# Expert stage of an audio-tower kernel: expert rows ordered by copy then expert, and the bias product cut to a quarter of the tokens per quarter tile

## The reference

```
gate_logits = x @ gate_w + gate_b
topk_vals, topk_idx = top_k(gate_logits, 2);  topk_w = softmax(topk_vals)
h = relu(einsum('bsh,ehf->bsef', x, w1) + b1)        # 16 experts x 128 hidden
expert_out = einsum('bsef,efh->bseh', h, w2) + b2
moe = sum over the two chosen experts of topk_w * expert_out
y = layernorm(x + moe) * gamma + beta
```

## Time and profile before

| | us |
|---|---|
| median of 3 runs (lowest, highest) | 782.41 (780.72, 784.95) |
| the profiled execution's own time | 780.68 |
| its span, first to last instruction | 778.5 |
| PE busy | 741.2 (95%) |
| PE weight loads busy | 435.2 (56%) |
| DVE busy | 579.5 (74%) |
| ACT busy | 492.1 (63%) |
| POOL busy | 459.6 (59%) |

### The profile page before, as it was taken

How to read it: one execution, slowest core, us unless ns; L and a number is a source line. 1 busy time by engine, 2 the same in 40 slices (tenths; PEclk the granted TensorE clock), 3 DMA queues, 4 the chain that set the end, 5 groups by cost and what they waited for, 6 DMA issues and landing times.

```text
span 778.5 us, 17037 instructions
## 1 busy us (share of the span) xinstructions
PE 741.2 (95%) x5712; PEld 435.2 (56%) x5712; DVE 579.5 (74%) x1474; ACT 492.1 (63%) x993; POOL 459.6 (59%) x620
## 2 busy tenths in 40 slices
PE   2999999999999999999999999999999999999994
PEld 1343356776667667676766666544555554454441
DVE  7676776677677676777767665788888888888864
ACT  1566777777767777777777777554554655545441
POOL 7645314654556445564446542367788788888885
PEclk9999999999999999999999999999999999999997
DMA  6300205455755466454664557000000000000000
GB/s 177 105 2 2 53 3 133 110 123 118 160 120 119 106 140 157 109 123 110 145 143 100 117 124 160 2 2 1 9 13 10 9 9 8 8 16 7 9 7 20
DMA packets 41820, 56.20 MB, mean 72 GB/s; under 512 B 16360, under 2 KB 40680, under 8 KB 41608
## 3 DMA queue, kind: packets, MB, share of 16 engines
q1 hardware_dynamic: 40744, 53.87, 30.0%
q10 hardware_dynamic: 992, 1.26, 0.6%
HBM read 5.06 MB, written 2.43 MB: 10 GB/s over the span
## 4 chain that ended last, share of the span: by engine, by line
PE 82%; DVE 4%; POOL 4%; issue 3%; SPq 3%; ACT 3%; DMA 2%; ACTq 0%; DVEq 0%; POOLq 0%
PE bank L1446 14%; PE bank L1424 13%; PE bank L1316 13%; PE bank L1274 10%; PE bank L1343 8%; PE bank L1345 6%; PE bank L1187 5%; PE bank L1278 2%; PE bank L1177 2%; DMA m<-s2o 1%; PE bank L1471 1%; SPq L333 1%; PE bank L1463 1%; PE bank L1230 1%; ACT cs L624 1%
## 5 line engine op out<-in xcount | busy, mean ns | idle before, releaser
L953 DVE TENSOR_SCALAR prob<-prob,cap_hi,cap_lo 125x500 f32<-125x500 f32 x256 | 152.6, 623 | 84.8 <-ACT prob L668 83.7
L478 POOL TENSOR_TENSOR sq<-sq 125x256 f32<-125x256 f32 x128 | 97.5, 773 | 194.2 <-ACT sq L632 172.3
L668 ACT ACTIVATE prob<-bank 125x500 f32<-125x500 f32 x256 | 149.6, 596 | 56.4 <-PE bank L1345 55.8
L1424 PE MATMUL bank<-cs,w_sb 64*64 64x500 f32 x1024 | 147.1, 580 | 2.2 <-DVE gated L1071 2.0
L1446 PE MATMUL bank<-gated,w_sb 64*64 64x500 f32 x1024 | 148.9, 588 | 0.0
L522 POOL TENSOR_TENSOR gated<-relu,wb 128x500 f32<-128x500 f32 x96 | 120.1, 1253 | 48.0 <-ACT relu L768 45.6
L1071 DVE SCALAR_TENSOR_TENSOR gated<-bank,nb,wb 128x500 f32<-128x500 f32 x160 | 114.8, 727 | 35.2 <-PE bank L1424 35.2
L768 ACT ACTIVATE relu<-bank,b_sb 128x500 f32<-128x500 f32 x96 | 64.7, 673 | 93.2 <-PE bank L1424 93.2
L1424 PEld LDWEIGHTS bank<-cs,w_sb 64*64 64x64 f32 x1024 | 53.1, 133 | 54.7 <-issue 48.2
L632 ACT ACTIVATE sq<-bank 125x512 f32<-125x512 f32 x128 | 75.3, 599 | 3.9 <-POOL sq L478 0.8
L1274 PE MATMUL bank<-wqku_hi,s 128*125 128x512 f32 x192 | 77.1, 401 | 0.0
(11 more groups left out here) (188 smaller groups left out, 1507.1 us busy)
## 6 DMA issues: line engine op xcount, KB each, us to landing
m1o<-cs SPq DMA_DIRECT2D x128, 125.0 KB, 2.4
m<-mlow SPq DMA_DIRECT2D x120, 125.0 KB, 2.3
m1e<-cs SPq DMA_DIRECT2D x112, 125.0 KB, 2.4
out<-res SPq DMA_DIRECT2D x15, 125.0 KB
w_sb<-in_w SPq DMA_DIRECT2D x1, 1024.0 KB
m1e<-m1e SPq DMA_DIRECT2D x8, 125.0 KB, 2.3
xa<-xparts SPq DMA_DIRECT2D x3, 281.2 KB
w_sb<-in_w SPq DMA_DIRECT2D x1, 512.0 KB
```

Source lines behind the costliest of these rows:

```text
L478: gp.tensor_tensor(sq2[q][:, :, :], sq[q][:, :, 0:D // 2], sq[q][:, :, D // 2:D], ALU.add)\
L668: act.activation(prob[v % PROBS][:, :, c, :], bank[5 + n % 3][0:T, 0:C].rearrange("p (h l) -> p h l", h=2), ACT.Exp).then_inc(b_exp, 1)
L953: dve.tensor_scalar(part, part, cap_hi[0:T, h:h + 1], cap_lo[0:T, h:h + 1], ALU.min, ALU.max)\
L1424: last = pe.matmul(up_bank(g)[cols, 0:C], w1_sb[rows, g, cols], cs1[q % 3][rows, :], start=True, stop=True)
```

## The change

The 128 rows of a group are ordered copy first, then expert: row 16r + e. That changes the layout of `w1`, `b1`, `w2` and `b2` on the host and the broadcast with which DVE writes `wtok`. At the end of the attention stage PE sums `b2f` once over the 8 copies, with a 0/1 matrix of 128 columns that is added to the table of constants. The result, `b2s`, has the full bias of the 16 experts in rows 0 to 15 and again in rows 64 to 79, and zeros in the other rows. In each half, the first 16 rows of `wb` hold the weights of the 16 experts once. Each half of the rows can now make the full bias product, so each of the four tiles gets a quarter of the tokens (125 columns): rows LO tokens 0 to 249, rows HI tokens 250 to 499.

```diff
-C_COLS = C_II + D
+C_SUM = C_II + D
+C_COLS = C_SUM + 128
...
+    for half in (0, HALF):
+        c[:, C_SUM + half:C_SUM + half + E] = np.tile(np.eye(E), (R, 1))
...
+        b2s = sb("b2s", [128, D])
-        wtok = sb("wtok", [T, CH, E, R])
+        wtok = sb("wtok", [T, CH, R, E])
...
 ACT, start_c:
+                if v == 2:
+                    act.wait_ge(c_bsum, 1)
+                    act.activation(b2s[:, :], bank[4][:, 0:D], ACT.Copy).then_inc(c_bias, 1)
...
 DVE, gate_step, n == 17:
-                    first, second = (lg[:, k, :, :].unsqueeze(3).to_broadcast([T, CH, E, R]) for k in (5, 6))
+                    first, second = (lg[:, k, :, :].unsqueeze(2).to_broadcast([T, CH, R, E]) for k in (5, 6))
                     done(dve.tensor_tensor(wtok[:, :, :, :], first, second, ALU.add))
...
 PE, start_c:
                 if v == 1:
                     pe.wait_ge(b_ev, 16 * PAIRS)
                     pe.wait_ge(b_gl, 4 * PAIRS)
+                    pe.matmul(bank[4][:, 0:D], c_sb[:, C_SUM:C_SUM + 128], b2f[:, :], start=True, stop=True)\
+                        .then_inc(c_bsum, 1)
+                    pe.wait_ge(b_gl, 4 * PAIRS)
                     tokens_c(0)
...
 PE, extra:
                 pe.wait_ge(c_wbs, q + 1)
-                for cols, part in ((LO, slice(0, L)), (HI, slice(L, C))):
-                    for rows, y in ((LO, bank[0]), (HI, bank[1])):
-                        pe.matmul(y[cols, part], b2f[rows, :], wb[q % 2][rows, part], start=False, stop=False,
-                                  skip_group_check=True)
+                if q == 0:
+                    pe.wait_ge(c_bias, 1)
+                for c, (cols, rows, y) in enumerate(((LO, LO, bank[0]), (HI, LO, bank[0]), (LO, HI, bank[1]), (HI, HI, bank[1]))):
+                    part = slice(c * T, (c + 1) * T)
+                    pe.matmul(y[cols, part], b2s[rows, :], wb[q % 2][rows, part], start=False, stop=False,
+                              skip_group_check=True)
...
 host:
-    w1 = a("L0_ffn_w1").reshape(E, D, G, R)
+    w1 = a("L0_ffn_w1").reshape(E, D, G, R).transpose(1, 2, 3, 0).reshape(D, G, 128)
...
-        "b1": a("L0_ffn_b1").reshape(E, G, R).transpose(0, 2, 1).reshape(128, G),
-        "w2": a("L0_ffn_w2").reshape(E, G, R, D).transpose(0, 2, 1, 3).reshape(128, G, D),
-        "b2": np.repeat(a("L0_ffn_b2"), R, axis=0),
+        "b1": a("L0_ffn_b1").reshape(E, G, R).transpose(2, 0, 1).reshape(128, G),
+        "w2": a("L0_ffn_w2").reshape(E, G, R, D).transpose(2, 0, 1, 3).reshape(128, G, D),
+        "b2": np.tile(a("L0_ffn_b2"), (R, 1)),
```

More of the change, by code:

```diff
@@ L173, in build @@
         s_wprod = sem("s_wprod")
+        c_bsum, c_bias = sem("c_bsum"), sem("c_bias")
         a_xin, a_split, a_scr, a_table = sem("a_xin"), sem("a_split"), sem("a_scr"), sem("a_table")
@@ L1471, in weights_c @@
                     last = pe.transpose(bank[3][:, c * T:(c + 1) * T],
-                                        wtok[:, c, :, :].rearrange("p e r -> p (e r)"), ident[0:T, 0:T])
+                                        wtok[:, c, :, :].rearrange("p r e -> p (r e)"), ident[0:T, 0:T])
                 last.then_inc(c_wt, 1)
@@ L1568 @@
         "gb": rows(a("L0_ffn_gate_b"), T),
-        "w1": np.tile(w1.transpose(1, 2, 0, 3).reshape(D, G, 128), (2, 1, 1)),
-        "b1": a("L0_ffn_b1").reshape(E, G, R).transpose(0, 2, 1).reshape(128, G),
-        "w2": a("L0_ffn_w2").reshape(E, G, R, D).transpose(0, 2, 1, 3).reshape(128, G, D),
-        "b2": np.repeat(a("L0_ffn_b2"), R, axis=0),
+        "w1": np.tile(w1, (2, 1, 1)),
+        "b1": a("L0_ffn_b1").reshape(E, G, R).transpose(2, 0, 1).reshape(128, G),
+        "w2": a("L0_ffn_w2").reshape(E, G, R, D).transpose(2, 0, 1, 3).reshape(128, G, D),
+        "b2": np.tile(a("L0_ffn_b2"), (R, 1)),
         "fg": rows(a("L0_ffn_gamma"), T),
```

## The result

The kernel after takes 787.73 us (median of 8 runs, 785.03 to 789.91), the kernel before 782.26 in 8 runs. The ratio is 1.0064, 95% interval 1.0044 to 1.0084. The forecast was 779.7 us, 776.8 to 782.8. The change makes the kernel slower by 5.5 us, not faster by 2.7.

A forecast was written before the change was run, and what follows sets the result against it. The prediction took PE to bound the steady expert stage. 14 pairs at 0.21 us gave -2.9 us, the larger table +0.2, together -2.7: 779.7 us against a median of 782.41, range 776.8 to 782.8.

The forecast's parts named there:

- The smaller `extra`: PE's bias product in the expert stage: half the columns, 0.21 us instead of 0.42, gaining 0.21 us a pair.
- rival (a): Expert stage: short `extra` instructions are limited by their weight loads; gain 0.15 us a pair, 780.7 us; chance 0.13.
- serial rival (d): Tiles of short `extra` don't overlap, weight loads run one after another: 0.64 us more a pair, 791 us; chance 0.02.
- The sum: Whole kernel: -2.9 us from the pairs plus 0.2 us at the start gives -2.7 us.
- the count of pairs: Expert stage: the gain reaches the end in 14 pairs, 1 to 13 and the last.
- The start, the new steps, the new order: Larger constants table costs 0.2 us at the start; new steps ending attention and the new row order cost zero.
- What is late next: Steady pairs: PE's third `up` behind `extra` keeps 0.12 us, the `wtok` transposes 0.45 us; cost taken as nothing.
- Rival (c): DVE and POOL collide in each steady pair, delaying PE's third `up` by 0.84 us: +7 us, 789.6; chance 0.05.
- The argument on pairs 0 and 14: PE stalls there behind `extra` (0.96 and 1.08 us) waiting for a bank DVE must read, so nothing is gained.

The follow-up runs named there:

- e3: The kernel after with DVE's two products of the gate's weights made one instruction of 128 elements; 779.35 us, ratio 0.9965.
- e8: The kernel after with one wait added: POOL's product of group 9 waits for DVE's second product of the gate's weights; 779.88 us, ratio 0.9965.
- e1: The kernel after with the bias product again full size (b2f, all 128 rows, 250 columns a tile), new layout kept; 781.66 us, ratio 0.9996.
- e2: The kernel before with the bias product over 125 columns a tile instead of 250, part left out, layout unchanged; 787.87 us, ratio 1.0072.
- e5: The kernel before with the bias product over 220 of 250 columns a tile, the rest left out; 781.21 us, one run.
- e6: The kernel before with the bias product over 195 of 250 columns a tile, the rest left out; 783.56 us, one run.
- e7: The kernel before with the bias product over 170 of 250 columns a tile, the rest left out; 787.03 us, one run.
- e9: The kernel after with DVE's second product of the gate's weights moved behind the gating of group 8; 781.58 us, ratio 0.9985.
- e4: The kernel before with DVE's two products of the gate's weights made one instruction; 782.08 us, ratio 1.0002.

## Why the prediction was wrong

**The smaller `extra`: right.** 0.21 us instead of 0.42 in each steady pair. The limit by weight loads (rival (a)) and the serial rival (d) are both out; so is, for tiles that run beside each other, the 81 ns a matmul (at 128 columns) that the Trainium skill gives in "TensorE: Matmul & The Clock Gate", section "Back-to-back issue gap", without saying for which tiles: eight instructions with 125 columns take 0.21 us, 26 ns each. The prediction had asked for 0.21 us in each tile. Of the first four instructions of that `up` three start 0.21 or 0.22 us sooner after `extra` than before and one only 0.08 (0.35 instead of 0.43). It costs nothing here: in e3 and e8 the last instruction of the third `up` starts 0.21 us sooner than in the kernel before (4.34 against 4.55 us after `extra`).

**The sum: right but for the collision.** e3 and e8, in which DVE's second product does not wait behind POOL's product, lie 2.5 and 2.7 us below the kernel before that ran beside them. The forecast was 2.7. The intervals reach from 1.4 to 4.1 us, but the profiles say it more closely: from the first `extra` to the end they are 3.1 and 3.3 us shorter than the kernel before, for a forecast of 14 x 0.21 = 2.9. So the gain in a pair and the count of pairs stand, and what is left is the step that failed.

**The start, the new steps, the new order: right or harmless.** 0.2 us was put down for the larger table. `c_sb` took 3.3 us to land instead of 3.2, and DVE's first step did not come later. e1, which has all of this, lies at 0.9996. `wtok`'s time did change, but by POOL's doing, as argued.

**"What is late next": the step that failed.** It cost the new slack at nothing, with 0.12 us to spare at the third `up`, and the sum counted on DVE keeping its timing: "DVE and POOL, from the middle of the pair, are behind and work through their queues without waiting for PE." That is true of DVE, and nearly true of POOL. But one step of POOL, its product of group 9, was released by ACT's relu, and that by PE's first `up` behind `extra`, the first thing that the change moves. In the kernel before it started at 575.97 us, 0.06 after POOL's sum had ended (574.66 + 1.25 = 575.91). DVE's second product came first by this gap. I had looked at the row and taken the gap for nothing: "POOL is still busy with L528 until 575.91 and takes its next product then, whether the relu comes earlier or not". POOL moved forward by only 0.12 us, but past DVE.

Rival (c) described just this mechanism, with 0.05 as its chance; what was put against it is the sentence quoted last. It also had the place, a gate step of DVE ahead of L1071, and its two first prices were nearly right: 0.96 us for the step and 0.84 for the third `up`. Its total, 789.6 us, was too high. What the runs show: the second product loses 1.28 - 0.21 = 1.07 us. PE's third `up` comes at 4.50 us after `extra` instead of the 3.57 of e3 and e8, 0.93 later. The transposes that follow are only 0.65 later. Without the stall the first four instructions of that `up` start spread over 0.35 us (in e3 at 3.57, 3.76, 3.91 and 3.92 us after `extra`); after the stall they start together, at 4.50 to 4.52. The last instruction of that `up` therefore starts only 0.65 us later (4.99 against 4.34), and the transposes follow it after 0.51 us in both kernels. 0.65 - 0.21 = 0.44 us a pair is what the period shows (16.98 - 16.54), and pairs 1 to 13 lose 0.43 to 0.46 each. From the first `extra` to the last it is 254.07 us after and 248.29 before, 5.8 more; the tail is 0.2 shorter. That is the measured 5.5 us.

**The argument on pairs 0 and 14: right.** Both keep their stalls (1.17 us against 0.96 in pair 0, 1.13 against 1.08 in pair 14). The period of pair 0 is 16.95 us in both kernels, that of pair 14 is 17.06 against 17.13.

What is shown and what is argued: that POOL's product ahead of DVE's is the cause is shown by e8 (order alone), e3 (one request) and e2 (nothing else changed), and the tipping by e5 to e7, with one run and one profile each. Which of the two gets the port when both are ready within 0.03 us is not settled by any run. e3 and e8 are faster than the kernel before by 0.35%, and so the only versions that beat both kernels clearly.

## What to carry to other kernels

When a step on the critical engine gets shorter, list what it releases on the other engines, and ask of each whether it now reaches a shared resource before something that used to slip in ahead of it; a gap of 0.06 us decided here over 1.07. A slack worked out with all other times held fixed says nothing if one of those times is an accident of order. Small operations of DVE with two SBUF inputs are best merged, or fenced by a wait on the POOL side, where the engine behind them has something that the bottleneck needs.

## What the runs showed of the hardware

A DVE instruction with two inputs in SBUF and a POOL instruction that reads SBUF were each served whole, and the one that came later waited. "SBUF — State Buffer" of the Trainium skill, section "SBUF: two separate sides", says this of a DVE operation with two SBUF inputs against a GpSimd operation that reads SBUF, and the runs agree. That a shared port is the reason is what the page says; the runs show only the waits. 64 elements took 0.21 us alone, 1.17 behind most of one POOL product and 1.28 behind a whole one. DVE's L1080 in e9, with one input in PSUM, ran in its usual 0.73 us at the same time as POOL's product. The price was set by the other engine's instruction, not by one's own size. In one place the order of the starts does not tell who waits: in e6 at 561.17 us POOL's product starts 0.02 us ahead of DVE's, and it is POOL's that takes longer (1.35 us), while DVE's takes its 0.21.

The part before the expert stage scatters by up to 2 us. Six kernels have the same program up to there (before, e2 and e4 to e7), and they reach the first `extra` between 506.90 and 508.90 us. A part of it is TensorE's clock. In the chain of waits eight instructions with 500 columns take 1.67 us at the lower level (1.2 GHz) and 0.84 at the upper (2.4 GHz); kernel before, then kernel after:

```profile
19.31 1.67 PE bank L1187 x8
...
22.94 0.84 PE bank L1187 x7
```

```profile
21.62 1.67 PE bank L1195 x8
...
25.38 0.84 PE bank L1195 x7
```

By the traces' record of the granted clock it rose to the upper level at 22.3 us in the kernel before and at 24.8 in the kernel after. In e3, a faster kernel, it was 24.6, in e8 22.7, and in e6, which has the start of the kernel before, 24.1, so this does not belong to the change. The two profiled spans differ by 7.2 us. Of these 1.4 arise in the first 31 us, 0.2 of them in a wait of PE for the read-back at 18.7 us, which e2 and e4 have as well. The spans alone would make the change look worse than the medians say.
